# Moving the recurrence of a decoder row half a row earlier: two key buffers, another order on four engines

## The chip, the core and the metric

The kernel runs on one core of a Trainium2 chip. TensorE multiplies matrices into PSUM banks, ScalarE (ACT) evaluates activation functions, VectorE (DVE) and GpSimd (POOL) do elementwise work, and SyncE (SP) issues the DMAs. Each engine runs its own program in order and waits on semaphores for the others. The metric is the device time of one execution in microseconds (us).

## What is computed

One layer of a decoder with three parts, each followed by a residual sum and a layer norm, on 8 rows of 256 tokens and 512 channels:

```python
x = _layernorm(x + attention(x))            # 16 heads, linear attention with decay, gated, over 2 x 1024 tokens
x = _layernorm(x + _wkv(time_decay, time_first, k=x, v=ctx_2048))
x = _layernorm(x + bitlinear(gelu(bitlinear(x, w_fc)), w_proj))   # ternary weights

def step(carry, kv_t):                      # _wkv: a recurrence over the 256 tokens of a row
    aa, bb, pp = carry
    ww = u + kt
    y_t = (e1 * aa + e2 * vt) / (e1 * bb + e2)
    new_carry = (e1b * aa + e2b * vt, e1b * bb + e2b, q2)
```

The change concerns the second and third part, which the kernel does one row after the other. For a row, the recurrence has two scans: `bb` (the denominator, from the exponentials of the keys) and `aa` (the numerator, from exponential times value). The output is `(aa + t2) / (bb + ek2)` plus the key.

## The kernel before

**Attention** runs first, as 64 units (16 heads by 4 groups of 512 tokens). A unit is projections, scores, mix and an output product. It takes about 1050 us and the change leaves its loops alone; only the last unit and what follows it are touched. The last unit also starts row 0 of the next stage.

**The row stage.** `row(b)` exists on four engines. On TensorE it is: the first product `fc` (two halves of the row, t = 0 and 1, of four groups of 8 matmuls each), `turn_h` (transposes of the hidden values, 4 at a time), the second product `proj(b, 0)` in two pieces, with `turn_back(b + 1)` (transposes the result of the next row's recurrence) between them, then `turn_x2(b + 1)` (the next row's normed input to the product), `turn_x1(b + 2)` (turns the input of the row after, which gives the key) and `proj(b, 1)`. There are 128 accumulating matmuls of 512 columns and 56 transposes in an ordinary row.

**The recurrence of row b + 1 beside row b.** ACT copies the turned input to the one buffer `key` (`copy_key(b + 2)`) at the end of row b and takes two sets of four exponentials, `ek1` and `ek2`. At the start of row b + 1 DVE scans `bb`; POOL multiplies `ek1` and `ek2` by the values (L1289, L1292; `weighted`), then adds the denominator (L1304); DVE scans `aa`; POOL adds the numerator (L1299); DVE takes two reciprocals (`invert`, L1058), each 512 elements wide, with `split_h(b, 0, 0)` (the low half of the split hidden values, L1068) between them; POOL multiplies and adds the key (`fraction`, L1311 and L1313, twice), after which `r_ok` lets `turn_back` go.

**Buffers that TensorE waits for.** `turn_h` writes two banks in turn, so the transposes of group j need `hq_lo` of group j - 2 from DVE (`hql_ok`). ACT's `gelu` frees the two banks of `fc` (`gelu_ok`), so group 3 of `fc` needs the first gelu.

**The input of later rows.** `input_sum(b)` (DVE) adds the scaled attention output to the loaded row in the one buffer `x1` and takes its statistics; POOL takes the inverse root (`root(NX, b)`), DVE the shift, and ACT normalises it (`input_norm`, L737). The attention's scale `rms` for rows 2 to 7 comes from `square_totals(1, GROUPS)` on TensorE, `mean_squares` on DVE (L1160) and a power on POOL (`rms_root`, L1271), once, just ahead of row 0.

Of the kernel before, what the change touches and what calls it, by code (L numbers as in the profile page):

```python
# [5 lines left out]
P = 128  # L6
# [9 lines left out]
HEADS, DH = 16, 128  # L16
# [20 lines left out]
def decoder_layer(nc, x_t, x_rows, ctx_t, w_heads, slopes, norm_w, decay, first, w_ffn, out):  # L37
# [6 lines left out]
    with ExitStack() as ctx:  # L44
# [85 lines left out]

        val = sb("val", [P, KT, SEQ], F32, ffn)
        key = sb("key", [P, KT, SEQ], F32, ffn)
        x2 = sb("x2", [P, 2, BT, HID], F32, ffn)
        y_out = sb("y_out", [P, BT, HID], F32, ffn)
        xq_hi = sb("xq_hi", [P, BT, KT, P], F16, ffn)
        xq_lo = sb("xq_lo", [P, BT, KT, P], F16, ffn)
        ek1 = sb("ek1", [P, KT, SEQ], F32, ffn)
# [7 lines left out]
        t2 = sb("t2", [P, KT, SEQ], F32, ffn)  # L145
        hid = sb("hid", [P, BT, INNER], F32, ffn)
        hq_hi = sb("hq_hi", [P, BT, FT, P], F16, ffn)
        hq_lo = sb("hq_lo", [P, BT, FT, P], F16, ffn)
        col_sum = sb("col_sum", [P, HID], F32, ffn)
# [6 lines left out]
        hssq = sb("hssq", [P, BT], F32, ffn)  # L156
        ffn.close()
# [69 lines left out]
        def _(sp):  # L227
# [71 lines left out]
            sp.wait_ge(projected, PROJ * (UNITS - 2))  # L299
# [18 lines left out]
        def _(pe):  # L318
# [73 lines left out]
            def turn_x1(b, to):  # L392
                pe.wait_ge(x1_ok, BT * b + BT)
                wait(pe, x2_ok, BT * b)
# [7 lines left out]
            def unit(h, g, lag1=True, lag2=True, fresh=False, final=False, turn=False):  # L402
# [10 lines left out]
                project(h, g, Q, fresh)  # L413
                if lag2:
# [3 lines left out]
                if turn:  # L418
                    pe.wait_ge(masked, 2 * u)
                    turn_x1(0, SC)  # L420
# [28 lines left out]
            def turn_back(b):  # L449
                pe.wait_ge(r_ok, 2 * b + 2)  # L450
                pe.wait_ge(key_ok, 2 * b + 2)
# [56 lines left out]
            def row(b, s, next_row=True, second_row=True):  # L508
                for f in range(4):
                    fc(b, 0, f)  # L510
                for f in range(4):
                    fc(b, 1, f)
                    turn_h(b, 0, f)
                proj(b, 0, 0, 2)
                if next_row:
                    turn_back(b + 1)
# [7 lines left out]
                if second_row:  # L524
                    turn_x1(b + 2, TR)
# [17 lines left out]
            for tt in range(4):  # L543
                output(HEADS - 1, U - 2, tt)
            column_sums()
            mix(U - 1)
            pe.wait_ge(evacuated, PROJ * U)
            turn_back(0)
# [6 lines left out]
            turn_x1(1, TR)  # L555
            pe.wait_ge(sq_added, U)
            pe.wait_ge(v_ready, U)
            square_totals(1, GROUPS)
# [832 lines left out]
```

## Time and profile before

| | us |
|---|---|
| median of 3 runs | 1427.16 (1426.18 to 1429.85) |
| the profiled execution, its own time | 1428.17 |
| its span, first to last instruction | 1426.3 |
| busy in the span: TensorE | 1357.1 (95%) |
| VectorE | 963.0 (68%) |
| ScalarE | 624.0 (44%) |
| GpSimd | 278.0 (19%) |
| mean granted TensorE clock | 0.983 of full speed |
| a load of a row or of its values, issue to landing | 3.3 |

The shares are means over two unlike stages. From about 1070 us on TensorE does the end of attention and the eight rows, and the other engines are busier than before. The chain of work that ended last runs through TensorE for 77% of the span, VectorE for 12%, ScalarE for 4% and GpSimd for 1%. In the row stage its pieces change from engine to engine all the time, so there the order of work on each of them matters. A wait can be read in two ways: as idle time of the engine that waits, and as the distance between the starts of the same instruction in successive rows.

### The profile page before, as it was taken

Reading aid. Unit: us, or ns where it says so; the run is one execution under the profiler, and the core shown is the slowest. Engines: PE = TensorE matmul, PEld = TensorE weight load, DVE = VectorE, ACT = ScalarE, POOL = GpSimd, SP = SyncE. Lnnn points to the kernel's source line nnn. Section 1 sums busy time; section 2 is a strip of 40 time slices with the busy share of each in tenths; the row PEclk is TensorE's granted clock in tenths of the full one; section 3 lists DMA queues with packets and bytes.
Section 4 is the critical chain, followed back from the end, with each engine's and each line's share of the span. In section 5 each row is a group of like instructions: output and inputs, shape, how many; then the busy total and the mean of one; then the engine's idle time right before and its main releaser. Section 6 shows DMA issues by size and latency. Waiting matters only on the chain.

```text
span 1426.3 us, 21107 instructions
## 1 busy us (share of the span) xinstructions
PE 1357.1 (95%) x6898; PEld 1059.0 (74%) x6898; DVE 963.0 (68%) x1710; ACT 624.0 (44%) x1184; POOL 278.0 (19%) x204
## 2 busy tenths in 40 slices
PE   7999999998999999999999999999994898998997
PEld 6888888887888888888888888888882544454443
DVE  5666666655666657666666766565669788888873
ACT  5433434342434343433434333434350676776754
POOL 2210101110101011110101110101115555444430
PEclk9999999999999999999999999999996999999999
DMA  5011111110111010111101010000000001111000
GB/s 200 6 47 52 59 37 59 45 66 23 45 37 44 22 44 22 44 35 38 44 22 44 22 44 8 30 7 29 23 30 15 31 30 45 45 44 45 15 16 30
DMA packets 14436, 55.02 MB, mean 39 GB/s; under 512 B 2112, under 2 KB 2112, under 8 KB 12096
## 3 DMA queue, kind: packets, MB, share of 16 engines
q1 hardware_dynamic: 14400, 54.55, 11.3%
q8 instruction: 21, 0.34, 0.1%
q14 instruction: 15, 0.12, 0.0%
HBM read 50.35 MB, written 4.19 MB: 38 GB/s over the span
## 4 chain that ended last, share of the span: by engine, by line
PE 77%; DVE 12%; issue 5%; ACT 4%; POOL 1%; DMA 0%; SPq 0%; ACTq 0%; DVEq 0%; POOLq 0%
PE bank L332 17%; PE bank L334 16%; PE bank L333 16%; PE bank L381 4%; PE bank L382 4%; PE bank L383 4%; DVE bb L1037 3%; DVE den L1058 2%; PE bank L347 2%; PE bank L363 2%; PE bank L371 2%; DVE aa L1050 1%; DVE stats L1001 1%; PE bank L344 1%; PE bank L345 1%
## 5 line engine op out<-in xcount | busy, mean ns | idle before, releaser
L332 PE MATMUL bank<-x_hi,w_hi 128*128 128x512 f32 x1024 | 413.7, 404 | 7.5 <-DVE x_lo L866 7.0
L334 PE MATMUL bank<-x_hi,w_lo 128*128 128x512 f32 x1024 | 401.5, 392 | 0.0
L333 PE MATMUL bank<-x_lo,w_hi 128*128 128x512 f32 x1024 | 400.4, 391 | 0.0
L851 DVE TENSOR_TENSOR resid<-resid,bank 128x512 f32<-128x512 f32 x256 | 173.4, 687 | 148.4 <-PE bank L383 148.4
L1251 POOL TENSOR_TENSOR sq_sum<-sq_sum,o_sq 128x512 f32<-128x512 f32 x64 | 104.3, 1630 | 858.0 <-ACT o_sq L608 858.0
L332 PEld LDWEIGHTS bank<-x_hi,w_hi 128*128 128x128 f32 x1024 | 193.4, 189 | 47.3 <-issue 9.2
L334 PEld LDWEIGHTS bank<-x_hi,w_lo 128*128 128x128 f32 x1024 | 193.1, 189 | 42.9
L333 PEld LDWEIGHTS bank<-x_lo,w_hi 128*128 128x128 f32 x1024 | 193.8, 189 | 36.7
L857 DVE SCALAR_TENSOR_TENSOR gated<-g_t,bank 128x512 f32<-128x512 f32 x64 | 44.0, 687 | 173.8 <-PE bank L363 173.8
L603 ACT ACTIVATE v_t<-bank 128x512 f32<-128x512 f32 x64 | 38.2, 597 | 182.9 <-PE bank L334 182.9
L381 PE MATMUL bank<-wo_hi,u_hi 128*128 128x512 f32 x256 | 101.7, 397 | 8.8 <-DVE resid L851 6.1
L603 ACT ACTIVATE q_t<-bank 128x512 f32<-128x512 f32 x64 | 38.3, 598 | 159.8 <-PE bank L334 159.6
L478 PE MATMUL bank<-tern,xq_hi 128*128 128x512 f16 x256 | 99.2, 388 | 2.2 <-ACT hid L701 1.8
L382 PE MATMUL bank<-wo_lo,u_hi 128*128 128x512 f32 x256 | 101.0, 394 | 0.0
L383 PE MATMUL bank<-wo_hi,u_lo 128*128 128x512 f32 x256 | 100.8, 394 | 0.0
L479 PE MATMUL bank<-tern,xq_lo 128*128 128x512 f16 x256 | 99.1, 387 | 0.0
L503 PE MATMUL bank<-tern,hq_hi 128*128 128x512 f16 x256 | 98.0, 383 | 0.0
L504 PE MATMUL bank<-tern,hq_lo 128*128 128x512 f16 x256 | 98.0, 383 | 0.0
L603 ACT ACTIVATE k_t<-bank 128x512 f32<-128x512 f32 x64 | 38.3, 598 | 116.5 <-PE bank L334 116.5
L608 ACT ACTIVATE o_sq<-bank 128x512 f32<-128x512 f32 x64 | 38.4, 601 | 102.8 <-DVE gated L857 102.8
L601 ACT ACTIVATE g_t<-bank 128x512 f32<-128x512 f32 x64 | 38.4, 599 | 85.9 <-PE bank L334 85.9
L1068 DVE SCALAR_TENSOR_TENSOR hq_lo<-bank,h_scale,hq_hi 128x512 f16<-128x512 f32 x64 | 45.7, 734 | 39.1 <-ACT hq_hi L745 39.1
(143 smaller groups left out, 2424.5 us busy)
## 6 DMA issues: line engine op xcount, KB each, us to landing
w_raw<-w_ffn SPq DMA_DIRECT2D x32, 512.0 KB, 3.3
raw<-w_heads SPq DMA_DIRECT2D x15, 1024.0 KB, 4.9
raw<-w_heads SPq DMA_DIRECT2D x17, 256.0 KB, 2.7
x_in<-x_rows SPq DMA_DIRECT2D x8, 512.0 KB, 3.3
val<-ctx_t SPq DMA_DIRECT2D x8, 512.0 KB, 3.3
out<-y_out SPq DMA_DIRECT2D x8, 512.0 KB, 2.6
resid<-x_t SPq DMA_DIRECT2D x3, 1024.0 KB, 9.2
resid<-x_t SPq DMA_DIRECT2D x4, 256.0 KB, 5.1
```

The costliest lines, as they stand in the source:

```text
L332: mm(PJ[j % 2][:, :], a, c, start=kt == 0, stop=False)
L333: mm(PJ[j % 2][:, :], a, d, start=False, stop=False)
L334: last = mm(PJ[j % 2][:, :], b, c, start=False, stop=kt == KT - 1)
L381: mm(YB[tt % 2][:, :], u_hi[:, c], wo_hi[:, :], start=True, stop=False)
L382: mm(YB[tt % 2][:, :], u_hi[:, c], wo_lo[:, :], start=False, stop=False)
L383: mm(YB[tt % 2][:, :], u_lo[:, c], wo_hi[:, :], start=False, stop=True).then_inc(y_done, 1)
L478: mm(FC[f % 2][:, :], xq_hi[:, t, kt, :], w, start=kt == 0, stop=False)
L479: last = mm(FC[f % 2][:, :], xq_lo[:, t, kt, :], w, start=False, stop=kt == KT - 1)
L503: mm(PR[t][:, :], hq_hi[:, t, k, :], w, start=k == 0, stop=False)
L603: fn(dst, src, ACT.Silu).then_inc(evacuated, 1)
L851: tt(resid[:, 4 * g + t, :], resid[:, 4 * g + t, :], YB[t % 2][:, :], ALU.add).then_inc(y_added, 1)
L1251: g_.tensor_tensor(sq_sum[:, g, :], sq_sum[:, g, :], o_sq[:, :], ALU.add).then_inc(sq_added, 1)
```

## The change

`key` becomes two buffers, used by even and odd rows. Everything of the recurrence moves ahead by about half a row:

- TensorE turns x1(b + 2) between the first and the second half of the first product of row b. For row 0 this place holds `square_totals` (moved behind the first half of the product), and x1(2) is turned at the old place.
- ACT norms x1(b + 2) at the start of row b, copies the key after the first four gelus, takes the first exponentials before `second_norm(b + 1)` and the second ones at the end of the row.
- DVE scans `bb` of row b + 2 ahead of `split_h(b, 1, 2)`, and starts a row with both reciprocals of row b + 1; the scan of `aa` stands between `split_h(b, 0, 0)` and `split_h(b, 0, 1)`. `input_sum` is one row further ahead (b + 3).
- POOL does the products and the denominator of row b + 2 at the end of row b.

Some declarations move so that buffers that begin early lie where attention has already finished. The core of the diff, first the buffers, the loads and TensorE:

```diff
-        key = sb("key", [P, KT, SEQ], F32, ffn)
+        key = sb("key", [P, 2, KT, SEQ], F32, ffn)
...
             with sp.Fori(1, BATCH - 3) as b:
...
                 load_ctx(ctx_row)
+                load_rows(x_row)
                 store(row_out)
-                load_rows(x_row)
...
-            def row(b, s, next_row=True, second_row=True):
+            def row(b, s, first=False, next_row=True, second_row=True):
                 for f in range(4):
                     fc(b, 0, f)
+                if first:
+                    pe.wait_ge(sq_added, UNITS)
+                    pe.wait_ge(v_ready, UNITS)
+                    square_totals(1, GROUPS)
+                    pe.wait_ge(gate_done, UNITS)
+                    pe.wait_ge(squared, UNITS)
+                elif second_row:
+                    turn_x1(b + 2, TR, BT * b + BT)
                 for f in range(4):
                     fc(b, 1, f)
...
                     turn_h(b, 0, f)
...
-                if second_row:
-                    turn_x1(b + 2, TR)
+                if first:
+                    turn_x1(b + 2, TR, 2 * BT)
                 proj(b, 1)
```

ScalarE's `row`:

```diff
+            def row(b, s, first=False, next_row=True, second_row=True):
+                if second_row and not first:
+                    input_norm(b + 2)
                 act.wait_ge(scfc_ok, b + 1)
                 for f in range(4):
                     gelu(b, 0, f)
                 mean(b, 0)
+                if second_row and not first:
+                    copy_key(b + 2, s, TR)
...
                 split_h(b, 1, 1)
+                if second_row and not first:
+                    exps1(b + 2, s)
                 if next_row:
-                    second_norm(b + 1)
+                    second_norm(b + 1, 1 - s)
...
+                if first:
+                    copy_key(b + 2, s, TR)
+                    exps1(b + 2, s)
                 if second_row:
+                    exps2(b + 2, s)
```

VectorE's `row`:

```diff
                 if not first:
                     summed = result(b - 1, 1, 1 - s)
                 if next_row:
-                    aa_states(b + 1)
+                    invert(b + 1, 0)
...
                 if next_row:
-                    invert(b + 1, 0)
+                    invert(b + 1, 1)
                 split_h(b, 0, 0)
                 if next_row:
-                    invert(b + 1, 1)
+                    aa_states(b + 1)
+                split_h(b, 0, 1)
...
+                if third_row and not first:
+                    input_sum(b + 3)
...
+                if second_row and not first:
+                    bb_states(b + 2)
                 split_h(b, 1, 2)
                 split_h(b, 1, 3)
...
                 after(result(b, 0, s))
                 bn(NO, 0, y_out[:, 0, :])
+                if first:
+                    bb_states(b + 2)
+                    input_sum(b + 3)
+                    shift(NX, b + 3)
```

GpSimd ahead of the rows, where `weighted` and `weighted_now` are the two products:

```diff
             rms_root(1, GROUPS)
+            root(NX, 2)
+            weighted(1)
+            denominator(1)
+            weighted_now(1)
+            row(0, 0, first=True)
```

**GpSimd, from the end of attention into row 0.** Before, `sq_sum` is the last sum of squares, `rms` the power for rows 2 to 7, the two lines `t<-ek,val` the products of row 1, then its denominator, its numerator and its fractions:

```order
L1281 TENSOR_TENSOR rstd_r<-var_r,neg_half 128x4
L1251 TENSOR_TENSOR sq_sum<-sq_sum,o_sq 128x512
L1271 TENSOR_TENSOR rms<-rms_in,neg_half 128x12
L1289 TENSOR_TENSOR t<-ek,val 128x1024
L1290 COPY aa<-val 128x4
L1292 TENSOR_TENSOR t<-ek,val 128x1024
L1304 TENSOR_TENSOR den<-bb,ek 128x1024
L1299 TENSOR_TENSOR num<-aa,t 128x1024
```

Of the change, at the same place (`rstd` is the inverse root for the input of row 2):

```order
L1314 TENSOR_TENSOR rstd_r<-var_r,neg_half 128x4
L1284 TENSOR_TENSOR sq_sum<-sq_sum,o_sq 128x512
L1304 TENSOR_TENSOR rms<-rms_in,neg_half 128x12
L1310 TENSOR_TENSOR rstd<-var_e,neg_half 128x2
L1322 TENSOR_TENSOR t<-ek,val 128x1024
L1323 COPY aa<-val 128x4
L1339 TENSOR_TENSOR den<-bb,ek 128x1024
L1327 TENSOR_TENSOR t<-ek,val 128x1024
L1334 TENSOR_TENSOR num<-aa,t 128x1024
```

The inverse root for row 2 now stands between the power and row 1's products, and the denominator stands ahead of the second product.

**VectorE, from the end of row 0 into row 1.** Before: the end of row 0 is the first half of its result and statistics, and row 1 begins with the scan of `bb` of row 2:

```order
L1106 SCALAR_TENSOR_TENSOR y_out<-col_sum,nmean,bank 128x512
L1109 SCALAR_TENSOR_TENSOR y_out<-y_out,sc_pr,x 128x512
L1001 BN_STATS stats<-y_out 128x6
L1203 UNCONDITIONAL_BRANCH
L1203 ISA
L1037 SCALAR_TENSOR_TENSOR bb<-ew,ek 128x255 x4
```

Of the change (`x<-resid,rms,x_in` to `nshift` is the input of row 3):

```order
L1132 SCALAR_TENSOR_TENSOR y_out<-col_sum,nmean,bank 128x512
L1135 SCALAR_TENSOR_TENSOR y_out<-y_out,sc_pr,x 128x512
L1027 BN_STATS stats<-y_out 128x6
L1063 SCALAR_TENSOR_TENSOR bb<-ew,ek 128x255 x4
L1050 SCALAR_TENSOR_TENSOR x<-resid,rms,x_in 128x512 x2
L1027 BN_STATS stats<-x 128x6 x2
L1031 BN_AGGR mv<-stats 128x2
L1035 TENSOR_SCALAR var_e<-mv 128x1
L1031 BN_AGGR mv<-stats 128x2
L1037 TENSOR_SCALAR var_e<-mv 128x1
L1042 SCALAR_TENSOR_TENSOR nshift<-mv,rstd 128x2
```

The scan and the whole input sum of row 3 have been put at the end of row 0.

**ScalarE, from the end of row 0 into row 1, in the change.** The last exponentials of row 2 are followed by the norm of row 3's input, and then by the first gelu (`hid`) of row 1; before, no norm stands there:

```order
L657 ACTIVATE ek<-key,u_min 128x256 x4
L806 UNCONDITIONAL_BRANCH
L806 ISA
L751 ACTIVATE x<-x,nshift,rstd 128x512 x2
L223 ISA
L714 ISA
L715 ACT_TABLE_LOAD
L715 ACTIVATE hid,hsum<-bank,sc_fc 128x512
```

The norm `x<-x,nshift,rstd` is now ahead of every gelu of row 1.

## Rows read from the trace of the kernel before

**Rows 1.** Timeline of TensorE, first matmul of rows 0, 1, 6, 7 (start, duration, instruction)

```profile
1112.16 0.38 PE L478 MATMUL bank<-tern,xq_hi 128*128 128x512 f16 x1 [0.41 <-issue]
...
1152.76 0.38 PE L478 MATMUL bank<-tern,xq_hi 128*128 128x512 f16 x1
...
1349.61 0.38 PE L478 MATMUL bank<-tern,xq_hi 128*128 128x512 f16 x1
...
1386.65 0.38 PE L478 MATMUL bank<-tern,xq_hi 128*128 128x512 f16 x1
```

**Rows 2.** Timeline of TensorE inside row 2: idle before in brackets

```profile
1207.25 0.63 PE L488 MATMUL bank<-ident,hid 128*128 128x128 f32 x4 [2.21 <-DVE hq_lo L1068]
...
1211.18 0.63 PE L488 MATMUL bank<-ident,hid 128*128 128x128 f32 x4 [1.57 <-DVE hq_lo L1068]
...
1215.10 1.04 PE L454 MATMUL bank<-ident,num 128*128 128x128 f32 x8
...
1223.04 1.09 PE L398 MATMUL bank<-ident,x 128*128 128x128 f32 x8 [0.63 <-ACT x L737]
```

**Rows 3.** Groups by shape, 1151 to 1381: busy us, mean ns, idle before

```profile
L1058 DVE RECIPROCAL den<-den 128x512 f32<-128x512 f32 x12 | 40.1, 3343 | 0.0
L1037 DVE TENSOR_TENSOR_SCAN bb<-ew,ek 128x255 f32<-128x255 f32 x24 | 39.9, 1723 | 2.2 <-ACT ek L641 2.1
L1068 DVE SCALAR_TENSOR_TENSOR hq_lo<-bank,h_scale,hq_hi 128x512 f16<-128x512 f32 x48 | 34.2, 734 | 18.8 <-ACT hq_hi L745 18.8
...
L1311 POOL TENSOR_TENSOR num<-num,den 128x512 f32<-128x512 f32 x12 | 15.2, 1268 | 15.5 <-DVE den L1058 15.5
...
L1050 DVE TENSOR_TENSOR_SCAN aa<-ew,t 128x255 f32<-128x255 f32 x24 | 14.5, 662 | 0.0
L1299 POOL TENSOR_TENSOR num<-aa,t 128x1024 f32<-128x1024 f32 x6 | 14.2, 2361 | 17.9 <-DVE aa L1050 17.9
...
L1277 POOL TENSOR_TENSOR rstd<-var_e,neg_half 128x2 f32<-128x2 f32 x17 | 11.9, 702 | 28.4 <-DVE var_e L1011 19.1 <-DVE var_e L1145 9.3
...
L641 ACT ACTIVATE ek<-key,u_neg 128x256 f32<-128x256 f32 x20 | 8.5, 496 | 0.1
...
L730 ACT ACTIVATE x<-bank,nshift,rstd_r 128x512 f32 x10 | 7.2, 774 | 10.7 <-DVE nshift L1088 10.7
...
L641 ACT ACT_TABLE_LOAD x5 | 6.4, 1283 | 0.1
...
L1281 POOL TENSOR_TENSOR rstd_r<-var_r,neg_half 128x4 f32<-128x4 f32 x6 | 6.0, 1008 | 13.0 <-DVE var_r L1079 13.0
...
L1290 POOL COPY aa<-val 128x4 f32<-128x4 f32 x6 | 3.5, 586 | 0.0
```

**Rows 4.** Timeline of VectorE in row 2: input sum, then second statistics

```profile
1213.23 1.41 DVE L1024 SCALAR_TENSOR_TENSOR x<-resid,rms,x_in 128x512 f32<-128x512 f32 x2
...
1216.56 1.42 DVE L1001 BATCH_NORM_STATS2 stats<-bank 128x6 f32<-128x512 f32 x2
```

**Rows 5.** Timelines of TensorE, VectorE and GpSimd, ahead of row 0

```profile
1108.14 1.03 PE L398 MATMUL bank<-ident,x 128*128 128x128 f32 x8
...
1092.96 2.75 DVE L1024 SCALAR_TENSOR_TENSOR x<-resid,rms,x_in 128x512 f32<-128x512 f32 x2
...
1111.79 0.17 DVE L1160 TENSOR_SCALAR rms_in<-bank 128x12 f32<-128x12 f32 x1 [2.56 <-PE bank L388]
...
1112.04 2.28 POOL L1271 TENSOR_TENSOR rms<-rms_in,neg_half 128x12 f32<-128x12 f32 x1 [8.72 <-DVE rms_in L1160]
```

**Rows 6.** Timeline of TensorE in row 0: third transposes, transposes of the recurrence

```profile
1129.41 0.63 PE L488 MATMUL bank<-ident,hid 128*128 128x128 f32 x4 [2.68 <-DVE hq_lo L1068]
...
1137.15 1.04 PE L454 MATMUL bank<-ident,num 128*128 128x128 f32 x8
```

**Rows 7.** Stretches of rows 2 and 3: length, busy of each engine, granted clock

```profile
1190.30:1229.50 39.20, 34.78 (x187) 18.75 (x185) 34.45 (x55) 27.86 (x54) 19.07 (x14) 1.00 0.12 41
1229.50:1269.90 40.40, 37.03 (x185) 19.46 (x183) 34.07 (x55) 27.34 (x52) 18.60 (x13) 0.92 0.11 39
```

More of the change, by code:

```diff
@@ L390, in square_totals, with turn_x1 @@
                 last.then_inc(sq_total, 1)
-            def turn_x1(b, to):
+            def turn_x1(b, to, read=0):
                 pe.wait_ge(x1_ok, BT * b + BT)
-                wait(pe, x2_ok, BT * b)
+                wait(pe, x2_ok, read)
                 for ct in range(KT):
@@ L413, in unit @@
                 project(h, g, Q, fresh)
+                if turn:
+                    pe.wait_ge(masked, 2 * u)
+                    turn_x1(0, SC)
                 if lag2:
@@ L542, in _ @@
             scores(U - 1, 1)
-            for tt in range(4):
+            pe.wait_ge(evacuated, PROJ * U)
+            turn_x1(1, TR)
+            for tt in range(2):
                 output(HEADS - 1, U - 2, tt)
             column_sums()
+            for tt in range(2, 4):
+                output(HEADS - 1, U - 2, tt)
             mix(U - 1)
-            pe.wait_ge(evacuated, PROJ * U)
-            turn_back(0)
+            turn_back(0, 2)
             for tt in range(2):
@@ L554, in _ @@
                 output(HEADS - 1, U - 1, tt)
[L555 to L558, printed above, removed]
-            pe.wait_ge(gate_done, U)
-            pe.wait_ge(squared, U)
-            pe.wait_ge(rms_in_ok, 2)
-            pe.wait_ge(y_added, 4 * U)
-            row(0, 0)
+            row(0, 0, first=True)
             with pe.Fori(0, (BATCH - 4) // 2) as i:
@@ L885, in unit @@
                 split_q(u)
+                if first_row:
+                    input_sum(1)
+                    dve.wait_ge(states0, 1)
+                    bb_states(0)
+                    early_input_norm(1)
                 if lag2:
@@ L1138, in row @@
                     root = second_shift(b + 1)
-                if second_row:
+                if third_row and not first:
+                    shift(NX, b + 3)
+                if first:
                     shift(NX, b + 2)
@@ L1153, in row @@
                 bn(NO, 0, y_out[:, 0, :])
+                if first:
+                    bb_states(b + 2)
+                    input_sum(b + 3)
+                    shift(NX, b + 3)
             def mean_squares(g0, g1):
@@ L1199, in _ @@
             dve.wait_ge(col_ok, 1)
+            input_sum(2)
             row(0, 0, first=True)
@@ L1312, in fraction, with row @@
                 pool.wait_ge(y_ok, 2 * b + half + 1)
-                g_.tensor_tensor(num[:, c, :], num[:, c, :], key[:, c, :], ALU.add).then_inc(r_ok, 1)
-            def row(b, first=False, next_row=True, second_row=True):
-                if next_row:
-                    weighted(b + 1)
-                    denominator(b + 1)
-                    numerator(b + 1)
+                g_.tensor_tensor(num[:, c, :], num[:, c, :], key[:, s, c, :], ALU.add).then_inc(r_ok, 1)
+            def row(b, s, first=False, next_row=True, second_row=True, third_row=True):
                 if not first:
@@ L1322, in row @@
                 if next_row:
-                    fraction(b + 1, 0)
-                    fraction(b + 1, 1)
-                if second_row:
-                    root(NX, b + 2)
+                    numerator(b + 1)
+                    fraction(b + 1, 1 - s, 0)
+                    fraction(b + 1, 1 - s, 1)
+                if third_row and not first:
+                    root(NX, b + 3)
                 if next_row:
@@ L1329, in row @@
                 root(NH, b)
+                if second_row:
+                    weighted(b + 2)
+                    denominator(b + 2)
+                    weighted_now(b + 2)
+                if first:
+                    root(NX, b + 3)
             root(NX, 0)
@@ L1334, in _ @@
             g_.memset(bb[:, :, 0:1], 1.0).then_inc(states0, 1)
+            root(NX, 1)
             denominator(0)
```

135 lines of the change are left out of this document (67 added, 68 removed).

## The prediction

> **What bounds the kernel now.** I first looked for the stages that TensorE does not fill. The first matmuls of the rows [rows 1] give their lengths: row 0 takes 1152.76 - 1112.16 = 40.60 us, rows 1 to 5 take (1349.61 - 1152.76) / 5 = 39.37 us each, row 6 takes 37.04 us. TensorE's own work in an ordinary row is much less. Between 1211.18 and 1215.10 it does four transposes and 16 matmuls [rows 2]. Eight transposes last 1.04 us there, 0.11 us from one to the next; so the 16 matmuls start every 0.216 us. 128 matmuls and 56 transposes make 33.8 us. So an ordinary row has about 5 us of waiting. [Rows 2] show where: 2.21 and 1.57 us ahead of `turn_h`, until `hq_lo` comes from VectorE, and 0.63 us ahead of `turn_x1`. `turn_back` at 1215.10 does not wait. [Rows 3] show what VectorE is late with: two reciprocals of 3.34 us and scans of `bb` that take 1.72 us each, where the same scan of `aa` takes 0.66. GpSimd multiplies during the first and not during the second.
>
> **Contention, as row and rule.** [Rows 3] alone give the price: four `bb` scans beside the two products cost 6.9 us, four undisturbed ones would cost 2.6. In their new place GpSimd has one product to do beside them, since the denominator behind it waits for the scans. I take half of the difference, 2.0, so 4.6 us. The Trainium skill, page "SBUF — State Buffer", section "Who interferes with whom", says that a VectorE instruction with two SBUF inputs and a GpSimd instruction that reads SBUF exclude each other for the whole length of the one that came first. The trace agrees (0.66 against 1.72 us). By that rule the price of a meeting is the rest of the other's instruction, at most 2.4 us here, which gives 4.6 again; without it the row would be 2 us shorter on VectorE.
>
> **The ordinary row after the change** (times from its first matmul). No operation is added; each is moved.
> - TensorE: half of `fc` 32 x 0.216 = 6.9, `turn_x1` 0.9 to 7.8, four groups with their `turn_h` 4 x 2.17 to 16.5, first piece of `proj` 3.45 to 19.95. It wants `turn_back` then.
> - VectorE: the row starts with the first row's result behind the products of GpSimd, at about 2.1; result 1.5, two reciprocals 6.5, statistics 1.1 end at 11.2. `hq_hi` of group 0 comes at 11.1 (turned at 10.0, one gelu ahead of it), `hq_lo` [rows 3] at 11.9, before TensorE needs it at 13.9. The 2.21 and 1.57 us waits go. The scan of `aa` ends at 14.2.
> - GpSimd then still has the numerator 2.36 and four fractions at 1.27 plus 0.07 between them [rows 3]: 14.3 + 2.36 + 5.3 = 22.0. Before, the reciprocals lay among the fractions and all of it ended before `turn_back`. Now `input_sum` falls on the fractions. Just this meeting is in [rows 5]: two sums took 2.75 us instead of 1.41 [rows 4]; I add 0.8 to the fractions. `turn_back` goes at 22.85: a new wait of 2.9 us.
> - From there: `turn_back` and two `turn_h` 1.75, second piece of `proj` 3.45, two `turn_h` 0.87, to 28.9. `second_norm` has to be done for `turn_x2`. The statistics (1.42 [rows 4] and six small operations, 2.1 in all) and the root, 1.0 [rows 3], come after the transposes, and the shift is ready at 27.3. But ACT now does the first exponentials ahead of it: table load 1.28 and 1.6 [rows 3], which end at 28.45. The norm's halves take 0.77 each: `turn_x2` goes at 29.25 and 29.95, and `proj(b, 1)` starts at 30.4, 0.6 us late.
> - VectorE scans `bb` from 28.6 for 4.6 us, beside a product, and only then does `split_h(b, 1, 2)`. Its `hq_lo` is there at 34.2, wanted at 33.85: 0.35 us. The row ends at 30.4 + 6.9 + 0.35 = 37.65.
>
> So of 5 us of waiting 3.9 come back at other places. Rows 1 to 4 save 39.37 - 37.65 = 1.7 each. Row 5 has no `input_sum` on its fractions: 36.9, saves 2.5. Row 6 has neither `turn_x1` nor exponentials: `turn_back` at 22.05, end at 35.9, saves 1.1. Together 10.5 us. Row 7 has no recurrence and is unchanged. The bounds of an ordinary row: 36.9 if nothing meets on the SBUF side, 39.4 if the late scans hold the norm's successors back fully.
>
> **The granted clock.** Row 3 ran at 0.92 of full speed in its stretch, row 2 at 1.00 [rows 7], with the same waits; a part of row 3 was at 1.2 GHz. Its stretch is 1.2 us longer than row 2's. The low level came behind waits. In the new row the long wait stands just ahead of `turn_back`, where the path has no slack. I add 2 us over the rows (bounds 0 and 6).
>
> **Ahead of row 0.** `turn_x1(1)` and `square_totals` leave the path between the last output and the first matmul: 1112.16 - 1108.14 = 4.0 us [rows 5, 1]. The recurrence of row 0 ends at about the same time, because `input_sum(1)` and its norm come into VectorE's queue ahead of `split_k` and `gate` of the last units, and cost what the earlier scan gives. Row 0 begins at 1108 (bounds 1106.8 and 1109.2).
>
> **Row 0 itself** is what decides. Times from its first matmul. `square_totals` now ends at 6.9 + 2.7 = 9.65 (2.7 is 1109.0 to 1111.75, ended by the row at 1111.79 [rows 5]). VectorE and the power on GpSimd, 2.28 [rows 5], to 12.2. VectorE's `input_sum(2)` waits for it: 3.33 [rows 4] to 15.6. In GpSimd's queue the inverse root for it, 0.70, and then row 1's product 2.35, the copy 0.59 and the denominator 2.35 [rows 3] follow: 21.75. VectorE's queue has `invert(1, 0)` and `invert(1, 1)` ahead of `split_h(0, 0, 0)`: 6.5 more, and `hq_lo` is there at 29.0. The third `turn_h` waits for it. Before, it ran at 1129.41 - 1112.16 = 17.25 [rows 6]. Scan of `aa` 2.34, numerator 2.36 and fractions 5.3 follow: `turn_back(1)` at 39.1, before at 24.99 [rows 6]. What before was hidden beside row 0 is serial here.
>
> **The start of row 1** waits again, since for row 0 x1(2) is turned at the old place and everything of rows 2 and 3 hangs on it. From 39.1: transposes and statistics to 42.4, root 43.5, `second_norm` 45.2, `input_norm(2)` 46.7, `turn_x1(2)` 47.8; on ACT the splits and the key to 49.75, table load 51.05, first exponentials 52.75. VectorE: scan of `bb` 4.6 to 57.35, then `input_sum(3)`, whose second half waits for the denominator on GpSimd, to 60.9, statistics 62.8. GpSimd has the second product until 63.25 and takes the root to 63.95. ACT has the norm of row 3 ahead of row 1's gelus: 65.65, table load 66.9, first gelu 67.85. TensorE came to row 1 at 54.5 and waits with group 2 of `fc`, which stands 3.45 into a row. Row 1 starts in effect at 67.85 - 3.4 = 64.45, before at 40.60: 23.85 us more.
>
> **The sum**, against the profiled execution of 1428.17: -4.1 (start of row 0) + 23.85 (rows 0 and 1) - 10.5 (rows 1 to 6) + 2 (clock) = +11.2, so 1439.4. The median of the runs shown is 1.0 lower; I say 1439. What lies outside the span is taken as equal. The second key buffer, the moved declarations and SP's new order I cost at nothing: `load_rows` comes ahead of `store`, each needed row is asked for more than 10 us ahead of its use and a load lands 3.3 us after its issue. If a load were late, its 3.3 us would stand in the row.
>
> **The rivals.**
> - *The rows run at TensorE's floor.* If the two waits went and nothing came back, six rows would take 33.8 and save 5.6, 5.6, 5.6, 5.6, 5.6 and 3.2, about 31 instead of 8.5: 1417. For it: VectorE's lateness is the only large wait in [rows 2]. Against it: 7.7 us of GpSimd work behind the scan of `aa` [rows 3] don't fit before 19.95.
> - *The chain through row 0 is not serial* (the other side). If the denominator of row 1 were ready before row 0 needs VectorE, the 11.7 us at the third `turn_h` and most of the stall in row 1 would be gone: 1439 - 20 = 1419. It decides where the products of row 1 stand behind the power in GpSimd's queue; the order rows say they do. The denominator would have to be ready 12 us earlier.
> - *Only row 1 is not held.* If row 3's norm came before TensorE needs the gelu, 10 us go: 1429, no change that can be told.
> - *The rows gain nothing.* The late scan of `bb`, ahead of two `split_h`, and the exponentials ahead of `second_norm` give rows of 39.4: 1439 + 8.5 = 1448.
>
> **How the numbers follow.** A measurement of this kernel can tell 0.3%, about 4.3 us. The forecast has 0.68, rows that gain nothing 0.08 (both slower), only row 1 not held 0.10 (the same), the serial chain absent 0.08 and the floor 0.06 (both faster). Slower 0.76, same 0.10, faster 0.14. The forecast's own range is 1433 to 1446: start of row 0 by 1.2, clock by 2 down and 4 up, rows 1 to 5 by 0.7 down. The range for 8 in 10 reaches to the unheld row 1 and to the rows without gain: 1425 to 1449.
>
> **What would show it.** The distance from row 0's first matmul to `turn_back(1)`: 39 us (25 would say that the chain is not serial). A wait of some 10 us ahead of group 2 of `fc` in row 1, released by ScalarE. Ordinary rows of 37.6 us with their long wait ahead of the transposes of `num` and no wait ahead of the third and fourth `turn_h`. Scans of `bb` of 4.6 us a row. The forecast is wrong if ordinary rows come near 34 us, or if row 0 stays near 41 us.

## The result

The changed kernel takes 1441.57 us (median of 4 runs, 1440.85 to 1442.74), the kernel before 1426.72 in the same series (4 runs, 1426.18 to 1429.85). The ratio is 1.010, with a 95% interval of 1.0083 to 1.0118: slower by 1%. 1439 was forecast, with a range of 1425 to 1449. The profiled run took 1441.0, with a span of 1438.8 (before 1428.17 and 1426.3).

The first matmuls of rows 0, 1, 2, 3 and 7 in the changed kernel, which answer to [rows 1] (columns: start, duration, engine, line, operation; L478 is the first product):

```profile
1107.61 0.39 PE L478 MATMUL bank<-tern,xq_hi 128*128 128x512 f16 x1
...
1162.11 0.38 PE L478 MATMUL bank<-tern,xq_hi 128*128 128x512 f16 x1
...
1212.59 0.38 PE L478 MATMUL bank<-tern,xq_hi 128*128 128x512 f16 x1
...
1250.26 0.38 PE L478 MATMUL bank<-tern,xq_hi 128*128 128x512 f16 x1
...
1399.17 0.38 PE L478 MATMUL bank<-tern,xq_hi 128*128 128x512 f16 x1
```

Row 0 begins 4.55 us earlier (1112.16 before). Then rows 0 and 1 take 104.98 us instead of 79.76, which is 25.2 more. Rows 2 to 6 take 186.58 instead of 194.73, which is 8.15 less; about 1.7 of that is the clock, since row 3 of the kernel before ran at 0.92 and took 40.66 us beside 38.95 for rows 2 and 4. Row 7 starts 12.5 us later, and so ends the span. The loss is all in the two rows that start the pipeline; the loop itself is faster.

The same in the table of busy time by stretch (columns: stretch and length, busy time and instructions of TensorE, its weight loads, VectorE, ScalarE and GpSimd, then the granted clock as a share of full speed, DMA share and GB/s), here rows 0 to 3:

```profile
1107.61:1162.11 54.50, 41.24 (x209) 22.86 (x209) 26.31 (x46) 26.01 (x50) 20.73 (x14) 0.84 0.06 20
1162.11:1212.59 50.48, 38.11 (x186) 20.63 (x185) 41.83 (x65) 29.97 (x55) 25.86 (x18) 0.86 0.09 32
1212.59:1250.26 37.67, 34.37 (x186) 18.69 (x185) 35.75 (x55) 27.25 (x52) 19.26 (x14) 1.00 0.11 43
1250.26:1287.94 37.68, 34.37 (x185) 18.64 (x184) 35.82 (x55) 27.24 (x52) 19.22 (x14) 1.00 0.11 42
```

Read the clock as well as the length: rows 0 and 1 ran at 0.84 and 0.86 (1.00 and 0.96 in the kernel before), rows 2 and 3 at full speed.

**The serial chain of row 0.** GpSimd, then VectorE, then TensorE in the timeline (in square brackets the idle time ahead and who ended it):

```profile
1118.21 2.28 POOL L1304 TENSOR_TENSOR rms<-rms_in,neg_half 128x12 f32<-128x12 f32 x1 [15.60 <-DVE rms_in L1193]
1124.02 0.69 POOL L1310 TENSOR_TENSOR rstd<-var_e,neg_half 128x2 f32<-128x2 f32 x1 [3.53 <-DVE var_e L1037]
1124.68 2.35 POOL L1322 TENSOR_TENSOR t<-ek,val 128x1024 f32<-128x1024 f32 x1
...
1127.11 2.34 POOL L1339 TENSOR_TENSOR den<-bb,ek 128x1024 f32<-128x1024 f32 x1
```

```profile
1129.49 6.56 DVE L1084 RECIPROCAL den<-den 128x512 f32<-128x512 f32 x2 [5.55 <-POOL den L1339]
1135.97 0.65 DVE L1094 SCALAR_TENSOR_TENSOR hq_lo<-bank,h_scale,hq_hi 128x512 f16<-128x512 f32 x1
1136.54 2.42 DVE L1076 TENSOR_TENSOR_SCAN aa<-ew,t 128x255 f32<-128x255 f32 x4
```

```profile
1136.77 0.44 PE L488 MATMUL bank<-ident,hid 128*128 128x128 f32 x1 [11.09 <-DVE hq_lo L1094]
...
1146.81 0.33 PE L454 MATMUL bank<-ident,num 128*128 128x128 f32 x1 [1.38 <-POOL num L1348]
```

The power begins 10.6 us into the row, the denominator ends at 21.8, the third `turn_h` runs at 29.2 (29.0 forecast) and `turn_back(1)` at 39.2 (39.1 forecast, 24.99 before).

**The stall of row 1.** GpSimd, VectorE, ScalarE and TensorE at the end of row 0:

```profile
1164.99 2.76 POOL L1339 TENSOR_TENSOR den<-bb,ek 128x1024 f32<-128x1024 f32 x1 [1.25 <-DVE bb L1063]
...
1170.47 0.70 POOL L1310 TENSOR_TENSOR rstd<-var_e,neg_half 128x2 f32<-128x2 f32 x1
```

```profile
1160.37 4.54 DVE L1063 TENSOR_TENSOR_SCAN bb<-ew,ek 128x255 f32<-128x255 f32 x4 [0.51 <-ACT ek L649]
1164.84 3.47 DVE L1050 SCALAR_TENSOR_TENSOR x<-resid,rms,x_in 128x512 f32<-128x512 f32 x2
```

```profile
1171.40 1.52 ACT L751 ACTIVATE x<-x,nshift,rstd 128x512 f32<-128x512 f32 x2 [9.46 <-DVE nshift L1042]
1172.94 1.28 ACT L715 ACT_TABLE_LOAD   x1
1174.23 0.69 ACT L715 ACTIVATE hid<-bank,sc_fc 128x512 f32<-128x512 f32 x1
```

```profile
1175.07 0.61 PE L478 MATMUL bank<-tern,xq_hi 128*128 128x512 f16 x1 [9.34 <-ACT hid L715]
```

Group 2 of `fc`, counted from 0 and so the third one, starts 67.46 us after row 0's first matmul; 67.85 was forecast. Later in the same row TensorE waits 2.81 us ahead of `turn_back`, and the granted clock in the stretches around and behind that wait is 0.79:

```profile
1194.00:1198.00 4.00, 1.47 (x7) 1.47 (x8) 3.14 (x7) 0.94 (x2) 2.96 (x3) 0.79 0.33 131
1198.00:1202.00 4.00, 4.00 (x21) 2.84 (x20) 2.91 (x13) 2.53 (x3) 1.07 (x2) 0.79 0.00 0
```

**An ordinary row** (row 3, the chain behind the scan of `aa` on GpSimd, and what TensorE waits for), to be read beside [rows 2] and [rows 3]:

```profile
1264.62 2.35 POOL L1334 TENSOR_TENSOR num<-aa,t 128x1024 f32<-128x1024 f32 x1 [5.45 <-DVE aa L1076]
1267.11 1.27 POOL L1346 TENSOR_TENSOR num<-num,den 128x512 f32<-128x512 f32 x1
1268.46 1.27 POOL L1348 TENSOR_TENSOR num<-num,key 128x512 f32<-128x512 f32 x1
1269.69 1.72 POOL L1346 TENSOR_TENSOR num<-num,den 128x512 f32<-128x512 f32 x1
1271.48 1.59 POOL L1348 TENSOR_TENSOR num<-num,key 128x512 f32<-128x512 f32 x1
```

```profile
1273.20 0.98 PE L454 MATMUL bank<-ident,num 128*128 128x128 f32 x7 [2.90 <-POOL num L1348]
...
1279.90 1.25 PE L463 MATMUL bank<-ident,x 128*128 128x128 f32 x8 [0.41 <-ACT x L744]
```

The waits of 2.21 and 1.57 us ahead of `turn_h` are gone, a wait of 2.90 has come ahead of `turn_back`.

### The profile page after: what moved, and what is told of

Read it like the earlier page. It is cut to its first block, busy times and chain, and to the rows that moved or that the text cites. A ratio compares the mean times of both kernels' runs of the same rounds, so it can differ in the third digit from the quotient of the medians.

```text
span 1438.8 us, 21064 instructions
## 1 busy us (share of the span) xinstructions
PE 1357.4 (94%) x6898; PEld 1059.9 (74%) x6898; DVE 963.9 (67%) x1711; ACT 620.7 (43%) x1182; POOL 278.8 (19%) x204
## 4 chain that ended last, share of the span: by engine, by line
PE 77%; issue 7%; POOL 6%; DVE 5%; ACT 4%; DMA 0%; SPq 0%; POOLq 0%; ACTq 0%; DVEq 0%
PE bank L332 16%; PE bank L334 16%; PE bank L333 16%; PE bank L381 4%; PE bank L382 4%; PE bank L383 4%; PE bank L347 2%; PE bank L363 2%; PE bank L371 2%; POOL num L1346 2%; POOL num L1334 1%; DVE den L1084 1%; POOL num L1348 1%; PE bank L344 1%; PE bank L345 1%
## 5 line engine op out<-in xcount | busy, mean ns | idle before, releaser
L478 PE MATMUL bank<-tern,xq_hi 128*128 128x512 f16 x256 | 100.3, 392 | 10.8 <-ACT hid L715 10.8
L848 DVE TENSOR_TENSOR probs<-bank,decays 128x256 f32<-128x256 f32 x128 | 53.4, 417 | 26.1 <-PE bank L347 24.1
```

The lines of the kernel that those rows point to most:

```text
L478: mm(FC[f % 2][:, :], xq_hi[:, t, kt, :], w, start=kt == 0, stop=False)
```

## Experiments

Two theories to begin with. *Serial start*: all of the loss lies in the chains of rows 0 and 1, and with a better order there the kernel is no slower than before. *VectorE is full*: it is busy for 35.8 of 37.7 us in a row, so the new order costs in itself, and time freed at the start is spent again. The experiments start from the changed kernel. Distances below are between first matmuls of rows, as above. Experiments 1, 3 and 6 to 10 are one run each, so their whole times say little below 2 us: in the profiles of experiments 3, 6 and 7, whose edits leave all that runs ahead of row 0 as it is, or nearly so, row 0 begins at 1108.80, 1106.27 and 1105.71 (1107.61 in the changed kernel). The readings rest on the rows.

**Experiment 1: GpSimd's products of row 1 ahead of the power.**

```diff
-            rms_root(1, GROUPS)
-            root(NX, 2)
             weighted(1)
             denominator(1)
             weighted_now(1)
+            rms_root(1, GROUPS)
+            root(NX, 2)
```

> Only GpSimd's queue ahead of row 0 is changed against the changed kernel: the two products and the denominator of row 1 stand ahead of the power for rows 2 to 7. Theory 'serial start' (the time is lost in rows 0 and 1, because VectorE's reciprocals of row 1 wait for GpSimd's products behind the power): the reciprocals start when the input sum of row 2 ends, about 5.4 us earlier, the distance from row 0's first matmul to the transposes of row 1's recurrence falls from 39.2 to about 33.8 us, the whole time by 5.4 us to about 1436. Theory 'VectorE is full' (the row order itself costs, and any time freed at the start is spent again by VectorE later): the distance falls, but row 1 gets longer by as much, and the time stays within 2 us of the changed kernel's 1441.6.

Measured 1439.58 us. The distance to `turn_back(1)` fell to 35.2 us, where the serial start named 33.8; row 0 fell from 54.5 to 50.5, but began 2.2 us later than in the changed kernel. The whole time, 2.0 us less, is at the edge of what the rival allows, but its sign is missing: row 1 takes 50.85 us, 0.4 more and not 4. The late beginning turned up again in experiments 2 and 4.

**Experiment 2: also VectorE's reciprocals of row 1 ahead of the mean squares.**

```diff
+            invert(1, 0)
+            invert(1, 1)
             mean_squares(1, GROUPS)
```

> As the run with GpSimd's queue alone, and VectorE takes the two reciprocals of row 1 ahead of the mean squares, beside TensorE's first half of row 0. Serial start: both pieces of the chain (7.6 us of GpSimd, 6.5 us of reciprocals) are hidden; hq_lo of row 0 comes as soon as the input sum of row 2 is done; the third transposes of hidden values run 18 us after row 0's first matmul instead of 29.2, the transposes of the recurrence 27.7 us after it instead of 39.2; the time falls by 11.5 us to about 1430. VectorE is full: less than 4 us are gained, 1437.5 or more.

Measured 1435.31 us (1432.03 to 1438.02), ratio to the kernel before 1.0062 (1.0049 to 1.0076). Row 0 takes 44.07 us, the gap ahead of the third `turn_h` is 0.75 instead of 11.09: the chain of row 0 was that. Row 1 still takes 50.5, with a gap of 9.35 ahead of group 2. The total fell between the two theories. The row began late again, because of these VectorE operations just ahead of it (from VectorE's timeline); behind them TensorE waits 2.60 us for VectorE's `resid`, and from the last transposes ahead of row 0 to its first matmul it takes 7.16 us instead of 4.03:

```profile
1101.57 2.20 DVE L1121 TENSOR_TENSOR sc_x<-sc_x,rstd_r 128x2 f32<-128x2 f32 x1
1103.81 2.40 DVE L1123 TENSOR_SCALAR sc_fc<-sc_x,w_fc_scale 128x2 f32<-128x2 f32 x1
```

Two operations on 2 elements, 0.16 and 0.23 us in the changed kernel, last 2.2 and 2.4 beside GpSimd's products. The Trainium skill, page "SBUF — State Buffer", section "Who interferes with whom", says that a VectorE instruction with two SBUF inputs contends with a GpSimd instruction that reads SBUF, and that the ports they share are an exclusive lock. L1121 agrees with it: it has two SBUF inputs and ends at 1103.77, and GpSimd's product runs from 1101.40 to 1103.75. The price here is the rest of the other's instruction and has nothing to do with the size of the one that waits.

**Experiment 3: only ScalarE, in row 1 alone the norm of row 3's input behind the gelus (for this, rows 1 to 4 are written out instead of looped).**

```diff
-                if second_row and not first:
+                if second_row and not first and not late:
                     input_norm(b + 2)
...
                 mean(b, 0)
+                if late:
+                    input_norm(b + 2)
```

> Only ScalarE is changed: in row 1 alone the norm of row 3's input stands behind the four gelus and the mean, not ahead of them (rows 1 to 4 are written out instead of looped). Serial start: the stall of 9.3 us ahead of group 2 of the first product of row 1 goes, a stall of about 4 us comes ahead of the transposes of x1(3), VectorE's reciprocals of row 2 are late by 1 to 2 us; row 1 gets 4 to 6 us shorter, 1436 to 1437.5. VectorE is full: VectorE's reciprocals of row 2 end at the same time as before, so the transposes of row 2's recurrence move by less than 2 us and the time is 1440 or more.

Measured 1445.62 us: a miss. The hold itself went, and the rival's sign did not come: `turn_back` of row 1 moved from 34.4 to 30.2 us into the row. The gap ahead of group 2 of `fc` is 0.51 instead of 9.34, a gap of 3.13 came ahead of the transposes of the late input, and row 1 fell from 50.48 to 46.21. But rows 2 to 6 took 7.6 us more. For one part the edit had a second effect. In the written-out program the table load stands behind the wait for the first product, so it is no longer hidden, and group 2 of `fc` waits 0.5 us in rows 1 to 4 too (rows 5 and 6 have this wait in the changed kernel as well). At full speed this made row 2 longer by 0.65 us. ScalarE's timeline in row 2:

```profile
1211.62 1.28 ACT L715 ACT_TABLE_LOAD   x1 [4.37 <-PE bank L479]
```

The larger part is the clock: rows 3 to 6 ran at 0.96, 0.92, 0.96 and 0.95, where the changed kernel has 1.00 (columns of the table of stretches; rows 2 and 4 of this kernel, between them row 3 with 39.18 us):

```profile
1209.62:1247.94 38.32, 34.55 (x185) 18.61 (x184) 35.84 (x55) 27.12 (x52) 19.25 (x14) 1.00 0.11 42
...
1287.12:1327.60 40.48, 37.11 (x186) 20.63 (x185) 36.30 (x55) 27.34 (x52) 19.50 (x14) 0.92 0.10 39
```

**Experiment 4: experiment 2, and at the end of row 0 the input sum of row 3 ahead of the scans of bb, its root ahead of GpSimd's products.**

```diff
+                if first:
+                    root(NX, b + 3)
                 if second_row:
                     weighted(b + 2)
...
-                if first:
-                    root(NX, b + 3)
```

> The early products and reciprocals of row 1, and at the end of row 0 the input sum of row 3 ahead of the scan of bb of row 2 (with its inverse root ahead of GpSimd's products). Serial start: 11.5 us from the first part; the stall in row 1 shrinks by about 7 us but VectorE's reciprocals of row 2 come 3.9 us later against the row, so 3.5 us net: 1426.5, about the kernel before. VectorE is full: the second part gains nothing, 1430 or more.

Measured 1430.46 us (1427.51 to 1432.9), ratio 1.0028 (1.0019 to 1.0037). The gap in row 1 is 4.25 us instead of 9.34. The number is the rival's (1430 or more), but the second part did gain: row 1 takes 45.8 us instead of 50.5. The trace has the remainder at the start, in two places: row 0 begins 2.3 us late as in experiment 2, and the shift that ScalarE's norm needs, 2 elements, takes 2.29 us beside the product that GpSimd has just begun.

**Experiment 5: the same, with the meetings of VectorE and GpSimd taken away at both places.**

```diff
+            pool.wait_ge(xql_ok, 2)
+            denominator(1)
             weighted(1)
-            denominator(1)
             weighted_now(1)
...
                     root(NX, b + 3)
+                    pool.wait_ge(shift_ok[NX], b + 2)
```

VectorE also takes `input_sum(3)` ahead of row 0's result.

> The start repaired as far as the traces show how: GpSimd's products of row 1 wait until VectorE has made the last low half for row 0's first product (two operations of 2 elements took 2.2 and 2.4 us beside them in the last kernel), the denominator first; at the end of row 0 the input sum of row 3 stands ahead of row 0's first result, and GpSimd's products of row 2 wait for that row's shift (2.29 us beside the product). Theory 'serial start': row 0 begins at 1107.6 and takes 44, group 2 of row 1's first product waits less than 1 us instead of 4.25, row 1 takes 39, row 2 begins at about 1190.7 (1191.92 in the kernel before), and five further rows of 37.5 to 38.5 give 1414 to 1420 us: faster than the kernel before by 0.5 to 0.8%. Rival 'the row order costs': the freed time is lost again later, as low clock or other waits, and the time stays within 0.3% of the kernel before (1422 to 1430).

Measured 1422.10 us (1421.08 to 1424.03), ratio 0.9966 (0.9955 to 0.9977). Row 0 begins at 1106.74 and takes 43.4; row 1 takes 43.9 instead of the 39 that I expected, because the denominator of row 2 is now what is late (1.51 us ahead of a `turn_h` and 3.83 ahead of `turn_back`). Rows 2 to 6 take 186.5 us, as in the changed kernel. The two small operations ahead of row 0 last 0.16 and 0.23 us again. The whole time is 2 us above what the serial start named and at the edge of the rival's range (1422 to 1430), so it does not decide. The rows do: the time came back where the start was mended and was not spent again in the later rows. The serial start holds, and VectorE being full is out as the cause of the loss. The same order that costs 1% is 0.3% faster than the kernel before with its first two rows put right.

**Experiment 6: the changed kernel with 33 matmuls more at the end of row 0** (into a bank that nobody reads).

```diff
                 proj(b, 1)
+                if first:
+                    for k in range(33):
+                        mm(HT[0][:, :], hq_lo[:, 0, 0, :], tern[:, 0, 0:512], start=True, stop=True)
```

> The changed kernel with 33 more matmuls of 512 columns at the end of row 0 on TensorE, into a bank that nobody reads; they stand in time in which TensorE waits anyway (9.34 us in row 1), so group 2 of row 1's first product starts at the same time. If the 3.3 us that row 1 takes beyond the sum are the price of the low clock after that wait, row 1 from group 2 on is 3 us shorter, its 16 matmuls take 3.6 instead of 5.67 us, and the time is 1438 to 1439. If they are another wait, row 1 ends as before: 1441 to 1442.

Measured 1442.86 us. A gap of 2.23 us was left, and behind it the matmuls ran at the low level all the same, 0.43 us apart instead of 0.22 (TensorE's timeline):

```profile
1173.73 0.45 PE L478 MATMUL bank<-tern,xq_hi 128*128 128x512 f16 x1 [2.23 <-ACT hid L718]
1173.97 0.63 PE L479 MATMUL bank<-tern,xq_lo 128*128 128x512 f16 x1
1174.39 0.63 PE L478 MATMUL bank<-tern,xq_hi 128*128 128x512 f16 x1
```

The time is no shorter for another reason besides. At the start of row 2 this kernel is 1.75 us ahead of the changed one, but rows 4 to 6 take 3.6 us more: they ran at 0.96, 0.96 and 0.95 instead of 1.00, with the same waits.

**Experiment 7: 43 matmuls, so that no gap is left.**

> As the kernel with 33 more matmuls at the end of row 0, but 43, so that TensorE has hardly any wait left ahead of group 2 of row 1's first product (2.23 us were left with 33, and the 16 matmuls behind it still took 5.31 us). If that wait brings the low clock, the 16 matmuls take 3.6 us now and row 1 is shorter by 2 to 3 us from there on. If they take over 5 us again, the low clock does not come from a wait right ahead of it.

Measured 1437.85 us. There is no gap, `fc` runs through, and row 1 takes 38.7 us, where the changed kernel takes 41.0 from its effective start, 3.45 us ahead of group 2. The granted clock of 1173.7 to 1178.8 in the two kernels, 33 first:

```profile
1173.70:1178.80 5.10, 5.07 (x16) 2.05 (x17) 5.03 (x7) 1.42 (x4) 0.70 (x1) 0.67 0.12 47
```

```profile
1173.70:1178.80 5.10, 5.10 (x29) 2.82 (x28) 5.02 (x7) 2.92 (x10) 0.70 (x1) 1.00 0.03 10
```

With the gap the stretch is at 1.2 GHz for most of the time, without it at 2.4. So the wait brings the low clock there, and it costs 2.3 us. Row 2 took 38.9 instead of 37.7 in this kernel, so half of what was gained was lost again. Of the 3.7 us in the whole time 1.9 are row 0 beginning earlier, which the edit does not touch.

**Experiment 8: no key added on GpSimd** (the output lacks that residual sum).

```diff
-                pool.wait_ge(y_ok, 2 * b + half + 1)
-                g_.tensor_tensor(num[:, c, :], num[:, c, :], key[:, s, c, :], ALU.add).then_inc(r_ok, 1)
```

> The changed kernel without the addition of the key to the fraction on GpSimd (two operations of 1.27 us in every row; the output is without the residual sum of the second part). If GpSimd's work behind the scan of aa sets the ordinary row, the 2.9 us wait ahead of the transposes of num goes nearly (below 0.5) and the ordinary row falls from 37.67 to 35.0 to 35.4. If VectorE, busy for 35.8 of 37.7 us, is the bound, the wait moves to its products and the row stays above 36.5.

Measured 1424.62 us. The ordinary row takes 36.28, between the two forecasts. The gap ahead of `turn_back` fell to 0.51, so the chain on GpSimd did set the row; but of 2.4 us only 1.4 are gained, since two waits for VectorE's late `hq_lo` take their place (TensorE's timeline in row 2):

```profile
1226.09 1.09 PE L454 MATMUL bank<-ident,num 128*128 128x128 f32 x8 [0.51 <-POOL num L1346]
...
1232.77 0.63 PE L488 MATMUL bank<-ident,hid 128*128 128x128 f32 x4 [0.82 <-DVE hq_lo L1094]
...
1238.36 0.38 PE L503 MATMUL bank<-tern,hq_hi 128*128 128x512 f16 x1 [0.63 <-DVE hq_lo L1094]
```

**Experiment 9: GpSimd's first product waits for all late scans of bb.**

```diff
-                wait(pool, scans_ok, 2 * KT * b)
+                pool.wait_ge(scans_ok, 2 * KT * b + KT)
```

> The changed kernel, with GpSimd's first product of a row waiting until VectorE has finished all four late scans of bb. If the scans take 4.56 us because of that product, they take 2.6 to 2.7 now; they are off the path that sets the row, so the ordinary row stays within 0.4 of 37.67. If the late scans do hold TensorE (the case of rows that gain nothing), the row falls by 1 us or more.

Measured 1439.89 us. The scans' group over rows 2 to 5, first in the changed kernel and then here (columns: count, busy us, mean ns):

```profile
L1063 DVE TENSOR_TENSOR_SCAN bb<-ew,ek 128x255 f32<-128x255 f32 x16 | 18.2, 1195 | 0.6 <-ACT ek L649 0.3
```

```profile
L1063 DVE TENSOR_TENSOR_SCAN bb<-ew,ek 128x255 f32<-128x255 f32 x16 | 9.8, 668 | 0.6 <-ACT ek L649 0.3
```

The row fell by 0.13, from 37.67 to 37.54. The late scans do not hold the row. What they free is idle time of VectorE ahead of the first `hq_lo`, 1.42 us.

**Experiment 10: the same, and the scan of aa in that idle time.**

```diff
+                if next_row:
+                    aa_states(b + 1)
                 split_h(b, 0, 0)
-                if next_row:
-                    aa_states(b + 1)
```

> The changed kernel with its start as it is; GpSimd waits for all late scans of bb, and VectorE scans aa ahead of the first low half. Against the kernel with the scans alone VectorE has 1.4 us of idle time ahead of that low half, so aa starts 2.1 us earlier. If what follows aa sets the row, ordinary rows fall from 37.54 to 35.5 to 36.4 us. If not, they stay above 37.

Measured 1426.31 us with the start as bad as ever (rows 0 and 1: 54.7 and 46.6). Ordinary rows take 35.36 to 35.73 us, and the gap ahead of `turn_back` is 0.39 to 0.76 (TensorE's timeline in row 2):

```profile
1229.26 0.98 PE L454 MATMUL bank<-ident,num 128*128 128x128 f32 x7 [0.39 <-POOL num L1348]
```

**Experiment 11: experiments 5 and 10 together**, with the denominator first on GpSimd in every row, and the first reciprocal ahead of the result on VectorE.

> The kernel with the repaired start, and in all rows: GpSimd starts its products only after VectorE's late scans of bb and takes the denominator first, VectorE scans aa ahead of the first low half and takes the first reciprocal ahead of the result of the row before. At the end of row 0 the scans of bb come ahead of that row's result. If GpSimd's work behind the scan of aa sets the ordinary row, the wait ahead of the transposes of num falls from 2.9 to below 1 us and rows 2 to 5 take 35.6 to 36.6 instead of 37.66: 1413 to 1418 us, 0.6 to 0.9% below the kernel before. If another chain has the same length (VectorE's own queue), rows stay above 37 and the time above 1419.

Measured 1410.10 us (1409.17 to 1410.33), ratio 0.9879 (0.9862 to 0.9895). Rows 2 to 4 take 36.6, one more than in experiment 10. GpSimd's queue shows why: the denominator needs the second exponentials, and the products behind it wait with it.

```profile
1220.77 2.36 POOL L1341 TENSOR_TENSOR den<-bb,ek 128x1024 f32<-128x1024 f32 x1 [2.90 <-ACT ek L657]
```

**Experiment 12: products first again** (the denominator first only at the two places around row 0; the result ahead of the reciprocal, a second difference from experiment 11).

> The repaired start of the kernel before with the loop of the kernel that scans aa first: in the last kernel of the series the denominator, taken first, waited 2.9 us for ScalarE's second exponentials in every row, and rows took 36.6 us, where products first gave 35.4 to 35.7. So GpSimd has its old order again in all rows but row 0, and VectorE the result ahead of the first reciprocal. If the wait for the exponentials is what cost, rows 2 to 4 take 35.4 to 35.8 and the time is 1404 to 1408 us (1410.1 with the denominator first). If it was hidden, and the new start is what holds the rows, they stay at 36.6 and the time at 1409 to 1411.

Measured 1406.71 us (1406.47 to 1407.55), ratio 0.9859 (0.9843 to 0.9876), the fastest of all and within its forecast: 20 us less than the kernel before in the same series, 35 less than the changed one in the first series. Ordinary rows take 35.7 us; what of the 0.9 us gained in each is the order on GpSimd and what the order on VectorE was not tried apart. The table of stretches for rows 0 to 3:

```profile
1105.62:1148.08 42.46, 38.61 (x210) 21.75 (x210) 27.08 (x52) 25.97 (x50) 20.08 (x14) 0.96 0.08 25
1148.08:1188.51 40.43, 36.04 (x185) 19.11 (x184) 36.15 (x61) 30.05 (x55) 24.31 (x18) 0.96 0.11 40
1188.51:1224.25 35.74, 34.16 (x185) 18.70 (x184) 31.80 (x55) 27.25 (x52) 18.77 (x14) 1.00 0.12 45
1224.25:1259.94 35.69, 34.17 (x185) 18.68 (x184) 31.69 (x55) 27.25 (x52) 18.71 (x14) 1.00 0.12 44
```

VectorE's busy time in a row is 31.8 instead of 35.8 us for the same instructions. The 4 us were time in which it was held beside GpSimd's work, which the profile shows as busy: 2.1 of them in the four scans of `bb` (mean 1196 ns before, 669 now), 1.6 in one shift of 2 elements (1.74 us in row 3 of the changed kernel, 0.15 here).

## Why the prediction was right, and where it was off

- **The sign and its cause** were right: what was hidden beside row 0 became serial. Forecast against measured from row 0's first matmul: third `turn_h` 29.0 and 29.2, `turn_back(1)` 39.1 and 39.2, end of row 0 54.5 and 54.5, group 2 of row 1 67.85 and 67.46. Experiments 2, 4 and 5 show it by taking it away, from 54.5 to 43.4 and from 50.5 to 43.9.
- **The start of row 0**: -4.1 forecast, -4.55 measured. That it came so near is partly luck, since this start moves by up to 3 us between kernels that are alike ahead of it (1105.71 to 1108.80).
- **The ordinary row**: 37.65 forecast, 37.67 to 37.68 measured, with the new wait at its forecast place (2.9 and 2.90). Row 5 was mis-sized, 36.9 against 37.53, 0.51 of it a wait ahead of group 2 of `fc` that I did not have; row 6 was 35.9 against 36.03. Of the parts, the scans of `bb` (4.6 and 4.56) and the fractions' 0.8 were met, the first better than its working: half of 6.9 - 2.6 is 2.15 and not 2.0, and 2.6 plus 2.4 by the rule is 5.0 and not 4.6. Alone the four scans take 2.45 us (experiment 9), so the meeting cost 2.1. Two parts were not met, and cancelled: `proj(b, 1)` does not wait 0.35 us for a low half, but starts at 30.7 instead of 30.4. `turn_x2` waits 0.41, not 0.6. Experiment 10 shows the chain behind `aa` as what sets the row. Experiment 8 shows a second one only 1.4 us shorter, so this order was near its end on two engines at once.
- **The clock** was the mis-sized term. "I add 2 us over the rows" was meant for the wait ahead of `turn_back`. Rows 2 to 4 wait 2.9 us there and run at 1.00, so in them it cost nothing in this trace. The low level came in row 1, from which the sum took no clock: from the effective start to row 2 it took 41.0 instead of 37.65, 3.3 more. Experiment 7 shows 2.3 us of it as the clock behind the stall. The rest is at the place that I named: in the 8 us around and behind row 1's wait of 2.81 us ahead of `turn_back` the clock was 0.79, and from that `turn_back` to the second piece of `proj` it took 3.34 us, which row 3 does in 1.80. Some 0.5 of this came back, as the wait ahead of `turn_x2` is not there.
- **The sum**: +11.2 forecast; the start of row 7, and with it the end, moved by 12.5. The differences by term: start -0.45, rows 0 and 1 +3.05 (22.15 forecast with row 1's saving, 25.2 measured), rows 2 to 6 +0.65, clock -2. These have both signs, so that the sum came within 1.3 is partly luck. The rest to the medians (+14.85) is that the profiled run of before lay 1.45 above this series' median and that of after 0.6 below, and that 0.3 more lies outside the spans.
- **The rival "only row 1 is not held"** was priced at 10 us. Experiment 3 removed the hold and row 1 fell by 4.3, since the late input then held the transposes and the low clock stayed. Its price was too high.
- **The rival of the other side** named its point: the denominator of row 1 ready 12 us earlier. Experiment 1 does that, and experiment 2 takes the reciprocals early too. Together they give 10 us in row 0, but not the 20 that I put on it, because the stall of row 1 has a cause of its own in the order at the end of row 0.

Open: why the same wait of 2.9 us ahead of `turn_back` is followed by full speed in rows 2 to 4 of the changed kernel and by the low level in row 1 of the same kernel, in row 2 of experiment 4 (0.96, 38.97 us) and in row 4 of experiment 6 (0.96, 38.51 us). The runs of that kernel spread over 5.4 us, those of the kernel before over 1.8 in the same series, and no run here tells what decides. Open too is how exactly experiment 3's loss divides, as it changed two things.

## What to carry to other kernels

A software pipeline that is deepened pays in the rows that fill it. Read the order of the peeled rows on every engine, and look for work of the next row that stands behind something new (here the reciprocals and products behind the power). The loop was faster from the start, 37.67 us a row instead of 39 to 40.7, and the two peeled rows hid it. When a wait moves, look for what else it frees: lifting the contention on `bb` gave 0.13 us a row by itself and some 2.1 together with the scan moved into the hole. Don't put an operation first because it is needed first when its own input is the last to come.

## What was unexpected of the hardware

- An operation on 2 elements on VectorE took 2.2 to 2.4 us instead of 0.2 beside a GpSimd product of 2.35 us, and TensorE reached row 0 some 3 us later for it (7.16 instead of 4.03 us behind the last transposes). Experiment 5, with GpSimd held back, has them at 0.16 and 0.23. The second of them, L1123, is a tensor-scalar with one tensor input and a column of scalars, and it was held as well. The same section of the Trainium skill, page "SBUF — State Buffer", "Who interferes with whom", lists tensor-scalar among the operations that can take the shared ports, by a mode of their own; this trace agrees for one of 2 elements.
- TensorE's low level (16 matmuls in 5.3 us instead of 3.6) followed a gap of 2.23 us in experiment 6, behind a stretch at 1.00. In experiment 5 a gap of 1.16 us ahead of the same matmuls did not bring it there. The same kernel code with the same waits (2.1 to 2.9 us ahead of `turn_back`) ran rows 4 to 6 at 1.00 in the changed kernel and at 0.95 to 0.96 in experiment 6, which is 3.6 us.
